# Swin block on one core: the second MLP layer in half precision, x in two tiles, K and Q ahead of the first MLP layer

## The chip, the core and the metric

The kernel runs on one NeuronCore of a Trainium2 chip. The core has five engines that work side by side and wait for each other through semaphores: TensorE (PE in the profile: matmuls and transposes; PEld is its weight load), VectorE (DVE), ScalarE (ACT), GpSimd (POOL) and SyncE (SP, which here only issues DMAs). Operands lie in SBUF, matmul results in eight banks of PSUM. The metric is the time of the program on the device in microseconds (us), the median of three runs.

## The reference

One Swin block with shifted windows, in float32: x is 32 images of 56 x 56 tokens with 128 channels.

```python
y = roll(layernorm(x) * g1 + b1, (-3, -3))                 # windows of 7 x 7 tokens, 16 heads of 8 channels
q, k, v = split(windows(y) @ qkv_w.T + qkv_b)
attn = softmax(q * 8**-0.5 @ k.T + rel_pos_bias + mask)
x1 = x + roll(unwindow((attn @ v) @ proj_w.T + proj_b), (3, 3))
h = gelu((layernorm(x1) * g2 + b2) @ fc1_w.T + fc1_b)     # 512 hidden channels, exact gelu
out = x1 + h @ fc2_w.T + fc2_b
```

## The kernel before

**Bands.** The work is cut into 128 bands (`STEPS`). A band is one row of 8 windows in two images: 7 x 112 = 784 tokens. Each tile holds a band, with tokens or channels on the partitions.

**Turns.** Every engine runs the same loop of turns, t = -2 to 130. In turn t it works on several bands at once, each in another stage: layernorm 1 of band t+2; transposed input, K and Q of band t+1, and the row maxima of its logits; V, logits, exp and the product with V of band t; attention output, projection, x1 and layernorm 2 of band t-1; the first MLP layer (fc1), gelu and four sevenths of the second (fc2) of band t-2; the last three sevenths of fc2 of band t-3. The order in a turn is written out by hand for each engine, and an engine never leaves it. A late operand therefore stops an engine and all that stands behind it.

**A turn on TensorE.** Transposes of z2 (L838), of the normalised x (L846) and of the maxima (L749). `fc2` of band t-3, rows 0 to 2 (L821). `fc1` chunks 0 and 1 (L805). K and Q (L867). `fc1` chunks 2 and 3. The spread of the softmax denominators (L881). V (L895). The projection (L904). Then the loop over eight windows w: `logits` (L771, L776), for even w `pv` (L791), for odd w one row of `fc2` (L821), and `max_logits` of the next band (L741), which with w = 0 waits for x1 (its PSUM banks 0 and 1 hold the projection until then) and with w > 0 for the maxima of w-1.

**Precision.** K, Q, V and fc1 use a split: a float32 operand is a high and a low float16 part, and three float16 products (high x high, low x high, high x low) replace one float32 product. fc2, the projection and the transposes are float32. Each float32 matmul shows as two passes, two records in the profile.

**VectorE in the middle of a turn.** `yT_lo` (L617, L621), the low part of the transposed x, which K and Q need; `sums` reciprocal (L630); the end of fc2 for three rows (L581); `norm1` of band t+2 (L521, L527), which waits for the x DMA; `k_lo` and `q_lo` (L641); `oT` (L657), attention output times the spread reciprocals; half of V into `v_own` (L672); x1 (L681) in two pieces; a second piece of V (L687); then the maxima (L589), one per window, with the statistics of layernorm 2 between them.

**ScalarE** makes `k_hi` and `q_hi` (L484), gelu (L438), two pieces of V (L500), exp (L421) and copies. **GpSimd** makes the low parts of the reciprocals (L372 to L378), the bias additions x_res (L384) and x1_b (L391), and both layernorms (`norm`, L350 to L361). **SyncE** issues the DMAs in order; x of band t+2 is loaded in turn t into the one tile `x_in`, after that tile's transposes.

The names k_hi, mx_k, st_q and so on in the rows are SBUF tiles; `ps` is PSUM.

Of the kernel before, what the change touches and what calls it, by code (L numbers as in the profile page):

```python
# [71 lines left out]
def swin_block_kernel(nc, x, wqT, wkT, wvT, wvpT, wpT, w1T, w2T, cols, rows, table_k, table_q, ident, eye,  # L72
# [11 lines left out]
    with ctx:  # L84
# [5 lines left out]
        w_2 = sb("w_2", [C, CH, C])  # L90
# [12 lines left out]
        x_in = sb("x_in", [TP, WS, C])  # L103
# [6 lines left out]
        z1, z2 = x_in, sb("z2", [TP, WS, C])  # L110
# [25 lines left out]
        hid = sb("hid", [C, CH, WS * TP])  # L136
# [4 lines left out]
        w_1, bv_wide = hid[:, 3, 0:HID], hid[:, 3, HID:HID + TP]  # L141
        w_q, w_k, w_v, w_vp = (oT_raw[:, k // 3, (k % 3) * C:(k % 3 + 1) * C] for k in range(4))
# [5 lines left out]
        def tokens_of(bank):  # L148
# [9 lines left out]
         s_h_lo, s_fc1, s_gelu, s_fc2, s_fin, s_stored, s_bd1, s_bd2, s_zero, s_init, s_initp, s_inita, s_bt,  # L158
# [11 lines left out]
                "h_high_ready", "h_low_ready", "fc1_done", "gelu_done", "fc2_done", "y_ready", "y_stored",  # L170
# [46 lines left out]
        def _(sp):  # L217
            band_dmas(sp, xr, x_in, 0, False, False, s_x)
# [30 lines left out]
            def body(t, edge, odd):  # L249
# [83 lines left out]
        def _(pool):  # L333
# [31 lines left out]
            def body(t, edge, odd):  # L365
                n = t - 1
                if exists(n):

                    pool.wait_ge(s_rsum, n + 1)
# [10 lines left out]
                    if n == 0:  # L380
                        pool.wait_ge(s_w, 16 * N_W)
                        pool.wait_ge(s_init, 2)
                    pool.wait_ge(s_xres_dma, loads(n, edge(n)))
                    nc.gpsimd.tensor_tensor(x_res[:, :, :], x_res[:, :, :],  # L384
                                            proj_b[:, :].unsqueeze(1).to_broadcast([TP, WS, C]),
                                            ALU.add).then_inc(s_xres, 1)
                n = t - 2
                if exists(n):
                    if past(n, 0):
                        pool.wait_ge(s_fin, 2 * n)  # L390
                    nc.gpsimd.tensor_tensor(x1_b[:, :, :], x1[:, :, :],  # L391
                                            fc2_b[:, :].unsqueeze(1).to_broadcast([TP, WS, C]),
                                            ALU.add).then_inc(s_x1b, 1)
                n = t + 2
                if exists(n):
                    norm(n, s_ln1, mv1, ve1, s_ve1, rs1, s_rs1, mr1, s_mr1, nm1, s_nm1, x_in, z1, s_t1, s_z1)
# [8 lines left out]
        def _(act):  # L405
# [27 lines left out]
            def gelu(n, c):  # L433
                if c == 0 and past(n, 0):
                    act.wait_ge(s_fc2, 2 * n)
                act.wait_ge(s_fc1, CH * n + c + 1)
                bank = 2 + 2 * (c % 2)
                nc.scalar.activation(hid[:, c, :].rearrange("p (b q) -> p b q", b=2), ps[:, bank:bank + 2, 0:HT],  # L438
                                     ACT.Gelu, bias=col[:, BF + c:BF + c + 1], scale=1 / W_SCALE).then_inc(s_gelu, 1)

            def body(t, edge, odd):
# [69 lines left out]
        def _(dve):  # L511
# [26 lines left out]
            norm1(0, lambda n: False)  # L538
# [21 lines left out]
            then(nc.vector.tensor_tensor(w1_lo[:, :], w_1, w1_hi[:, :], ALU.subtract))  # L560
            then(nc.vector.tensor_tensor(proj_b[:, :], proj_b[:, :], bp_ps, ALU.add))
# [33 lines left out]
            def body(t, edge, odd):  # L595
# [37 lines left out]
                n = t + 2  # L633
                if exists(n) and n != 0:
                    norm1(n, edge)
                n = t + 1
                if exists(n):
                    for j, (hi, lo, bank, b) in enumerate(((k_hi, k_lo, 0, BK), (q_hi, q_lo, 6, BQ))):
# [5 lines left out]
                        last.then_inc(s_lo, 1)  # L644
                n = t - 1
                if exists(n):
# [11 lines left out]
                    for im in range(2):  # L658
# [6 lines left out]
                        r[:, :, last_w, :, kept:WS].rearrange("p m i j -> p i m j")).then_inc(s_oT, 1)  # L665
                n = t
# [37 lines left out]

        @block.tensor
        def _(pe):
# [102 lines left out]
            def fc2(n, p, i):  # L809
                first, end = FC2_PARTS[p]  # L810
                if i == first and p == 1:
                    pe.wait_ge(s_gelu, CH * (n + 1))
                    if exists(n + 2):
                        pe.wait_ge(s_vown, 2 * (n + 2) + 1)
                        pe.wait_ge(s_vown_b, 2 * (n + 2) + 1)
                    elif n > 0:
                        pe.wait_ge(s_fin, 2 * n)
                if i == first and p == 0:
                    pe.wait_ge(s_fin, 2 * n + 1)
                for c in range(CH):  # L820
                    last = mm(ps[0:TP, 7, (i - first) * C:(i - first + 1) * C], hid[:, c, i * TP:(i + 1) * TP], w_2[:, c, :],  # L821
                              start=(c == 0), stop=(c == CH - 1))
# [3 lines left out]
            def body(t, edge, odd):  # L826
# [14 lines left out]
                if exists(n):  # L841
# [3 lines left out]
                    for i in range(WS):  # L845
                        last = nc.tensor.transpose(tokens_of(0)[:, i, 0:TP], z1[:, i, :], idn[0:TP, 0:TP])  # L846
# [22 lines left out]
                if exists(t - 2):  # L869
                    fc1(t - 2, 2)  # L870
# [108 lines left out]
```

## Time and profile before

| | |
|---|---|
| three runs | 4095.21 us (4090.11 to 4104.3) |
| the profiled execution | 4095.41 us, its span 4093.6 us |
| PE busy | 3947.3 us (96%), granted clock 0.995 |
| DVE busy | 2855.1 us (70%) |
| ACT busy | 2674.9 us (65%) |
| POOL busy | 2002.3 us (49%) |
| DMA | 35.6% of the 16 engines' time in the main queue |

PE shows 96% busy, but matmuls are pipelined, so the start times of matmuls in a turn, and not the busy share, tell how much time each piece occupies. The three other compute engines have idle time in each turn; what they cost is read where PE waits for them.

### The profile page before, as it was taken

The page shows a single profiled execution, that of the slowest core. Times are in us where ns is not written, and L with a number is a line of the kernel's source. Part 1 is how long each engine was busy: PE and PEld are TensorE (multiplying, and loading weights), DVE is VectorE, ACT ScalarE, POOL GpSimd, SP SyncE. Part 2 cuts the span into 40 slices and gives each one's busy share as a digit, 9 for nine tenths or more (in the row PEclk, how much of TensorE's full clock was granted, in tenths as well). Part 3 has the DMA queues.
Part 4 walks back from the last instruction along what each step waited for, and adds up shares of the span by engine and source line. Part 5 has one row for each costly group of instructions (what it writes and reads, how often), then busy time and mean ns, then how long its engine had stood idle before and what let it go on. Part 6 is the DMA issues. An engine that isn't in the chain of part 4 may idle for free. (4 is left out here: it accounts for less than half of the span.)

```text
span 4093.6 us, 168809 instructions
## 1 busy us (share of the span) xinstructions
PE 3947.3 (96%) x72080; PEld 3111.1 (76%) x72080; DVE 2855.1 (70%) x7453; ACT 2674.9 (65%) x3712; POOL 2002.3 (49%) x3476
## 2 busy tenths in 40 slices
PE   3899999999999999999999999999999999999998
PEld 2677777777777777777777777777777777777776
DVE  6677677677767777776776776777777667677764
ACT  1666666666666666666766666666666666666664
POOL 4454545445455454544544544454454445445453
PEclk8999999999999999999999999999999999999999
DMA  2333333333333333333333333333333333333332
GB/s 77 100 108 115 109 109 112 110 105 112 114 106 110 113 111 110 111 113 105 112 114 105 110 114 110 109 111 108 108 109 117 106 109 112 112 105 109 112 109 60
DMA packets 609568, 441.49 MB, mean 108 GB/s; under 512 B 142083, under 2 KB 608371, under 8 KB 608819
## 3 DMA queue, kind: packets, MB, share of 16 engines
q1 hardware_dynamic: 608355, 428.88, 35.6%
q8 instruction: 569, 9.32, 1.0%
q0 software_dynamic: 464, 1.81, 0.2%
q14 instruction: 180, 1.47, 0.1%
HBM read 106.14 MB, written 51.46 MB: 38 GB/s over the span
## 5 line engine op out<-in xcount | busy, mean ns | idle before, releaser
L589 DVE TENSOR_REDUCE neg_max<-ps 113x16 f32<-113x784 f32 x1024 | 995.9, 973 | 760.7 <-PE ps L741 760.5
L421 ACT ACTIVATE probs<-ps 113x784 f32<-113x784 f32 x1024 | 844.6, 825 | 858.4 <-PE ps L776 855.7
L821 PE MATMUL ps<-w,hid 128*112 128x128 f32 x7168 | 933.5, 279 | 1.9 <-ACT hid L438 1.0
L821 PEld LDWEIGHTS ps<-w,hid 128*112 128x112 f32 x7168 | 818.4, 177 | 81.9 <-issue 79.4
L776 PE MATMUL ps<-st_q,st_k 128*49 128x196 f16 x8192 | 696.2, 249 | 0.0
L771 PE MATMUL ps<-bias,eye_k 106*64 106x392 f16 x4096 | 686.5, 331 | 0.0
L438 ACT ACTIVATE hid<-ps,col 128x784 f32<-128x784 f32 x512 | 468.1, 915 | 165.4 <-PE ps L805 144.2
L741 PE MATMUL ps<-mx_k,mx_q 128*49 128x196 f16 x8192 | 544.2, 253 | 31.7 <-DMA mx_q<-q_hi 20.0
L350 POOL TENSOR_SCALAR ve<-mv 112x7 f32<-112x7 f32 x256 | 54.4, 212 | 1048.4 <-DVE mv L527 903.1
L776 PEld LDWEIGHTS ps<-st_q,st_k 128*49 128x49 f16 x8192 | 446.9, 105 | 122.0 <-issue 0.5
L372 POOL TENSOR_SCALAR r_hi<-sums 128x98 f16<-128x98 f32 x128 | 36.5, 285 | 897.9 <-DVE sums L630 897.9
L791 PE MATMUL ps<-probs,v_own 113*32 113x49 f32 x32768 | 464.4, 209 | 1.8 <-issue 1.5
L791 PEld LDWEIGHTS ps<-probs,v_own 113*32 113x32 f32 x32768 | 393.2, 110 | 83.6 <-issue 82.8
L741 PEld LDWEIGHTS ps<-mx_k,mx_q 128*49 128x49 f16 x8192 | 313.1, 103 | 152.1 <-DMA mx_q<-q_hi 33.1
L361 POOL TENSOR_SCALAR x_in<-x_in,rs,nm 112x128 f32<-112x128 f32 x896 | 389.5, 451 | 13.5 <-POOL nm L356 0.4
L361 POOL TENSOR_SCALAR z<-x,rs,nm 112x128 f32<-112x128 f32 x896 | 388.5, 449 | 13.4 <-POOL nm L356 0.3
L352 POOL TENSOR_TENSOR rs<-ve,half 112x7 f32<-112x7 f32 x256 | 380.4, 1486 | 21.3
L429 ACT ACTIVATE pv_sb<-ps 128x392 f32<-128x392 f32 x512 | 255.6, 499 | 203.9 <-PE ps L791 192.4
L414 ACT ACT_TABLE_LOAD x253 | 324.6, 1283 | 4.5
L521 DVE BATCH_NORM_STATS2 st<-x_in 112x6 f32<-112x128 f32 x896 | 185.9, 279 | 201.8 <-DMA x_in<-in_x 201.8
L384 POOL TENSOR_TENSOR x_res<-x_res,proj_b 112x896 f32<-112x896 f32 x128 | 267.2, 2088 | 10.3
L391 POOL TENSOR_TENSOR x_b<-x,fc_b 112x896 f32<-112x896 f32 x128 | 267.1, 2087 | 5.6 <-DVE y_out L581 5.6
(109 smaller groups left out, 6502.4 us busy)
## 6 DMA issues: line engine op xcount, KB each, us to landing
st_k<-k_hi SPq DMA_DIRECT2D x256, 196.0 KB
st_q<-q_hi SPq DMA_DIRECT2D x1024, 49.0 KB
oT_raw<-pv_sb SPq DMA_DIRECT2D x256, 196.0 KB, 3.6
x_in<-in_x SPq DMA_DIRECT2D x224, 196.0 KB
x_res<-in_x SPq DMA_DIRECT2D x224, 196.0 KB
out_y<-y_out SPq DMA_DIRECT2D x224, 196.0 KB
mx_k<-k_hi SPq DMA_DIRECT2D x512, 49.0 KB
mx_q<-q_hi SPq DMA_DIRECT2D x128, 196.0 KB
```

The lines of the kernel that those rows point to most:

```text
L352: nc.gpsimd.tensor_tensor(rs[:, :], ve[:, :], half[:, :], ALU.pow).then_inc(s_rs, 1)
L361: last = nc.gpsimd.tensor_scalar(z[:, i, :], src[:, i, :], rs[:, i:i + 1], nm[:, i:i + 1], ALU.mult, ALU.add)
L384: nc.gpsimd.tensor_tensor(x_res[:, :, :], x_res[:, :, :], proj_b[:, :].unsqueeze(1).to_broadcast([TP, WS, C]), ALU.add).then_inc(s_xres, 1)
L414: nc.scalar.activation(scrap[:, :], col[0:1, 0:1], function)
L421: nc.scalar.activation(probs[0:KP, w % 4, :].rearrange("p (b c) -> p b c", b=2), ps[0:KP, b:b + 2, 0:HB * WT], ACT.Exp).then_inc(s_exp, 1)
L438: nc.scalar.activation(hid[:, c, :].rearrange("p (b q) -> p b q", b=2), ps[:, bank:bank + 2, 0:HT], ACT.Gelu, bias=col[:, BF + c:BF + c + ...
L589: nc.vector.tensor_reduce(neg_max[0:KP, :, :, w].rearrange("p e g -> p g e"), ps[0:KP, 0:2, :].rearrange("p b (g c) -> p (b g) c", g=2)[:, ...
L741: last = mm(group(im, 0, g, 256), mx_q[edge(n)][:, g, span], mx_k[:, g, :, span], start=True, stop=True)
L771: mm(ps[HP * im:HP * (im + 1), bank + b, 0:HB * WT], eye_k[0:BIAS_ROWS, kind, im, :], bias[0:BIAS_ROWS, b, :], start=True, stop=False)
L776: last = mm(group(im, bank, g, EQ * WT), st_k[par][:, g, span], st_q[par][:, :, g, span], start=False, stop=(g % 2 == 1))
L791: last = mm(ps[32 * r:32 * r + VC, 6, first:first + WT], v_own[0:KP, w, h, :], probs[0:KP, w % 4, h * WT:(h + 1) * WT], start=True, stop=True)
L821: last = mm(ps[0:TP, 7, (i - first) * C:(i - first + 1) * C], hid[:, c, i * TP:(i + 1) * TP], w_2[:, c, :], start=(c == 0), stop=(c == CH ...
```

## The change

Five edits.

1. fc2 goes to half precision. Set-up splits w_2 (scaled by 64) into `w2_hi`, `w2_lo`. After each gelu chunk VectorE casts it to `hid_hi` (`hid_high`, four casts of 128 x 784 in a turn) and GpSimd subtracts to give `hid_lo` (four subtractions). TensorE does 12 float16 matmuls per row of fc2 where it did 4 float32 ones. The last step (`finish`) multiplies by 1/64 as it adds.
2. The float32 gelu output now shares its buffer with `probs`, the exp output, so exp of windows 0 to 3 waits for `hid_lo`.
3. K and Q move ahead of all four fc1 chunks on TensorE; on ScalarE all four gelus follow `k_hi` and `q_hi`.
4. x is held in two tiles and loaded a turn earlier (band t+3 in turn t). Its statistics move from the middle of the VectorE turn to the maxima of windows 4, 5 and 6, its moments to the end of the turn.
5. The second piece of V moves from VectorE to ScalarE, behind exp of window 0. On GpSimd the addition to x_res moves to the front of the turn.

```diff
-        w_2 = sb("w_2", [C, CH, C])
+        w2_hi, w2_lo = (sb(n, [C, CH, C], F16) for n in ("w2_hi", "w2_lo"))
-        x_in = sb("x_in", [TP, WS, C])
+        x_in = [sb(f"x_in{e}", [TP, WS, C]) for e in range(2)]
-        hid = sb("hid", [C, CH, WS * TP])
+        hid_hi, hid_lo = (sb(n, [C, CH, WS * TP], F16) for n in ("hid_hi", "hid_lo"))
+        hid = probs
...
 # SyncE
-                n = t + 2
-                if exists(n) and n != 0:
-                    sp.wait_ge(s_t1, n)
-                    band_dmas(sp, xr, x_in, n, edge(n), False, s_x)
+                n = t + 3
+                if exists(n):
+                    sp.wait_ge(s_st1, n)
+                    if past(n, 1):
+                        sp.wait_ge(s_t1, n - 1)
+                    band_dmas(sp, xr, x_in[odd(3)], n, edge(n), False, s_x)
...
 # GpSimd, after x1_b and ahead of norm of band t+2
+                n = t - 2
+                if exists(n):
+                    for c in range(CH):
+                        pool.wait_ge(s_hid_hi, CH * n + c + 1)
+                        nc.gpsimd.tensor_tensor(hid_lo[:, c, :], hid[:, c, :], hid_hi[:, c, :],
+                                                ALU.subtract).then_inc(s_hid_lo, 1)
...
 # ScalarE
+                if w < CH and exists(n - 2):
+                    act.wait_ge(s_hid_lo, CH * (n - 2) + w + 1)
...
+                        if w == 0:
+                            nc.scalar.activation(v_place(0, 1), v_made(0, 1), ACT.Copy).then_inc(s_vown_b, 1)
...
 # VectorE
+            then(nc.vector.tensor_scalar(w_2, w_2, W_SCALE, None, ALU.mult))
+            then(nc.vector.tensor_copy(w2_hi[:, :, :], w_2))
+            then(nc.vector.tensor_tensor(w2_lo[:, :, :], w_2, w2_hi[:, :, :], ALU.subtract))
...
+            def hid_high(n, c):
+                dve.wait_ge(s_gelu, CH * n + c + 1)
+                if c == 0 and past(n, 0):
+                    dve.wait_ge(s_fc2, 2 * n)
+                nc.vector.tensor_copy(hid_hi[:, c, :], hid[:, c, :]).then_inc(s_hid_hi, 1)
...
-                n = t + 2
-                if exists(n) and n != 0:
-                    norm1(n, edge)
...
 # VectorE, after q_lo
+                if exists(t - 2):
+                    hid_high(t - 2, 0)
+                    hid_high(t - 2, 1)
...
 # VectorE, after oT
+                if exists(t - 2):
+                    hid_high(t - 2, 2)
+                    hid_high(t - 2, 3)
...
 # TensorE, fc2
-                for c in range(CH):
-                    last = mm(ps[0:TP, 7, (i - first) * C:(i - first + 1) * C], hid[:, c, i * TP:(i + 1) * TP], w_2[:, c, :],
-                              start=(c == 0), stop=(c == CH - 1))
+                for c in range(CH):
+                    for w_part in (w2_hi, w2_lo):
+                        mm(row, hid_hi[:, c, i * TP:(i + 1) * TP], w_part[:, c, :],
+                           start=(c == 0 and w_part is w2_hi), stop=False)
+                for c in range(CH):
+                    if i == first and p == 1:
+                        pe.wait_ge(s_hid_lo, CH * n + c + 1)
+                    last = mm(row, hid_lo[:, c, i * TP:(i + 1) * TP], w2_hi[:, c, :], start=False, stop=(c == CH - 1))
```

The order on TensorE after fc2 of band t-3, first before the change (L805 is fc1, two chunks; L867 is K and Q):

```order
L821 MATMUL ps<-w,hid 112x128 x11
L805 MATMUL ps<-h_hi,w_hi 128x392 [waits h_low_ready]
L805 MATMUL ps<-h_hi,w_hi 128x392
L805 MATMUL ps<-h_lo,w_hi 128x392 x2
L805 MATMUL ps<-h_hi,w_lo 128x392 x2
L805 MATMUL ps<-h_hi,w_hi 128x392 [waits exp_done]
L805 MATMUL ps<-h_hi,w_hi 128x392
L805 MATMUL ps<-h_lo,w_hi 128x392 x2
L805 MATMUL ps<-h_hi,w_lo 128x392 x2
L867 MATMUL ps<-yT_hi,wk_hi 128x392 [waits y_low_ready]
```

and the same place after it (L860 is the end of fc2, L902 is K and Q, L837 is fc1):

```order
L860 MATMUL ps<-w_hi,hid_lo 112x128 x4
L902 MATMUL ps<-yT_hi,wk_hi 128x392 [waits y_low_ready]
L902 MATMUL ps<-yT_hi,wk_hi 128x392
L902 MATMUL ps<-yT_lo,wk_hi 128x392 x2
L902 MATMUL ps<-yT_hi,wk_lo 128x392 x2
L902 MATMUL ps<-yT_hi,wq_hi 128x392 [waits y_ready,neg_maxT_ready]
L902 MATMUL ps<-yT_hi,wq_hi 128x392
L902 MATMUL ps<-yT_lo,wq_hi 128x392 x2
L902 MATMUL ps<-yT_hi,wq_lo 128x392 x2
L837 MATMUL ps<-h_hi,w_hi 128x392 [waits h_low_ready]
```

K and Q, with their wait for `yT_lo`, now stand directly behind fc2; the 12 matmuls of two fc1 chunks that stood between them are behind Q.

VectorE from q_lo to the first maxima, before (L657 is oT, L672 and L687 are pieces of V, L681 is x1):

```order
L641 SCALAR_TENSOR_TENSOR q_lo<-ps,col,q_hi 128x8x49
L657 TENSOR_TENSOR oT<-oT_raw,ps 128x7x49 [waits projected,r_spread,o_in]
L657 TENSOR_TENSOR oT<-oT_raw,ps 128x7x49
L657 TENSOR_TENSOR oT<-oT_raw,ps 128x14x4
L657 TENSOR_TENSOR oT<-oT_raw,ps 128x14x3
L672 COPY v_own<-ps 49x512 [waits v_projected,pv_done]
L681 TENSOR_TENSOR x<-ps,x_res 112x512 [waits projected,x1_biased,x_res_biased]
L681 TENSOR_TENSOR x<-ps,x_res 112x384 [waits projected]
L687 COPY v_own<-ps 49x512 [waits v_projected,x1_ready]
L589 TENSOR_REDUCE neg_max<-ps 113x4x4 [waits max_transposed,max_logits_ready]
```

and after (L604 is hid_high, `probs` is the buffer of the gelu output):

```order
L604 CAST hid_hi<-probs 128x784 [waits fc2_done,gelu_done]
L604 CAST hid_hi<-probs 128x784 [waits gelu_done]
L678 TENSOR_TENSOR oT<-oT_raw,ps 128x7x49 [waits projected,r_spread,o_in]
L678 TENSOR_TENSOR oT<-oT_raw,ps 128x7x49
L678 TENSOR_TENSOR oT<-oT_raw,ps 128x14x4
L678 TENSOR_TENSOR oT<-oT_raw,ps 128x14x3
L604 CAST hid_hi<-probs 128x784 [waits gelu_done] x2
L696 COPY v_own<-ps 49x512 [waits v_projected,pv_done]
L705 TENSOR_TENSOR x<-ps,x_res 112x512 [waits projected,x1_biased,x_res_biased]
L705 TENSOR_TENSOR x<-ps,x_res 112x384 [waits projected]
L610 TENSOR_REDUCE neg_max<-ps 113x4x4 [waits max_transposed,max_logits_ready,x1_ready]
```

Two casts stand ahead of oT and two between oT and x1; the piece of V behind x1 is gone from this engine.

GpSimd in a turn after the change:

```order
L377 TENSOR_TENSOR x_res<-x_res,proj_b 112x896 [waits x_res_loaded]
L383 TENSOR_SCALAR r_hi<-sums 128x98 [waits r_rows_in,r_sums_ready]
L386 TENSOR_TENSOR sums<-sums,r_hi 128x98 [waits r_high_ready]
L389 TENSOR_SCALAR r_lo<-sums 128x98 [waits r_rest_ready]
L395 TENSOR_TENSOR x_b<-x,fc_b 112x896 [waits y_ready]
L402 TENSOR_TENSOR hid_lo<-probs,hid_hi 128x784 [waits hid_high_ready] x4
L354 TENSOR_SCALAR ve<-mv 112x7 [waits moments1_done]
```

The four subtractions stand between x1_b and layernorm 1, where there was nothing before.

## Rows read from the trace of the kernel before

**Rows 1.** Source view of L749; columns: engine, form, count, ns min/median/max, first and last start.

```profile
L749 PE MATMUL ps<-idn,neg_max x128: 262/262/395, 81.6 to 4024.6; 113*128 113x113 f32 x128
```

**Rows 2.** Timeline of one turn, PE; columns: start, us, engine, line, operation, count, idle before.

```profile
2002.91 0.26 PE L749 MATMUL ps<-idn,neg_max 113*128 113x113 f32 x1
2002.91 2.68 PEld L821 LDWEIGHTS ps<-w,hid 128*112 128x112 f32 x24
...
2005.53 0.21 PEld L805 LDWEIGHTS ps<-h_hi,w_hi 128*128 128x128 f16 x2
...
2007.62 0.50 PE L867 MATMUL ps<-yT_hi,wk_hi 128*128 128x392 f16 x2
...
2009.67 0.49 PE L805 MATMUL ps<-h_hi,w_hi 128*128 128x392 f16 x2
...
2010.66 0.49 PE L805 MATMUL ps<-h_hi,w_hi 128*128 128x392 f16 x2
...
2011.75 0.50 PE L881 MATMUL ps<-r_rows,sel 32*128 32x392 f16 x2
2012.28 0.10 PEld L895 LDWEIGHTS ps<-wv_hi,yT_hi 128*128 128x128 f16 x1 [0.42 <-DVE q_lo L641]
...
2013.58 1.58 PEld L904 LDWEIGHTS ps<-w_p,oT 128*112 128x112 f32 x14
...
2015.29 0.11 PEld L771 LDWEIGHTS ps<-bias,eye_k 106*64 106x64 f16 x2
...
2016.12 0.33 PEld L741 LDWEIGHTS ps<-mx_k,mx_q 128*49 128x49 f16 x8 [0.18 <-issue]
...
2017.29 0.93 PEld L821 LDWEIGHTS ps<-w,hid 128*112 128x112 f32 x8 [0.16 <-issue]
...
2018.35 0.30 PEld L741 LDWEIGHTS ps<-mx_k,mx_q 128*49 128x49 f16 x8
...
2033.56 0.26 PE L749 MATMUL ps<-idn,neg_max 113*128 113x113 f32 x1
```

**Rows 3.** Waits in total: who waited for what, us, times, longest.

```profile
DVE st L521 <- DMA x_in<-in_x: 201.8, 128, 2.8
```

**Rows 4.** Timeline of the same turn, DVE.

```profile
2005.26 0.34 DVE L621 TENSOR_TENSOR yT_lo<-ps,yT_hi 128x56 f16<-128x56 f32 x2
...
2010.03 1.13 DVE L641 SCALAR_TENSOR_TENSOR k_lo<-ps,col,k_hi 128x392 f16<-128x392 f32 x2
2011.08 1.15 DVE L641 SCALAR_TENSOR_TENSOR q_lo<-ps,col,q_hi 128x392 f16<-128x392 f32 x2
2012.34 1.17 DVE L657 TENSOR_TENSOR oT<-oT_raw,ps 128x343 f32<-128x343 f32 x4
2013.42 1.06 DVE L672 COPY v_own<-ps 49x512 f32<-49x512 f32 x1
2014.85 1.16 DVE L681 TENSOR_TENSOR x<-ps,x_res 112x512 f32<-112x512 f32 x2 [0.36 <-PE ps L904]
```

**Rows 5.** Timeline of the same turn, ACT.

```profile
2006.89 1.85 ACT L438 ACTIVATE hid<-ps,col 128x784 f32<-128x784 f32 x2 [1.10 <-PE ps L805]
...
2008.93 0.93 ACT L484 ACTIVATE k_hi<-ps,col 128x784 f16<-128x784 f32 x1 [0.19 <-PE ps L867]
```

**Rows 6.** Timeline of the same turn, POOL.

```profile
2009.59 2.09 POOL L391 TENSOR_TENSOR x_b<-x,fc_b 112x896 f32<-112x896 f32 x1
...
2014.22 3.04 POOL L361 TENSOR_SCALAR x_in<-x_in,rs,nm 112x128 f32<-112x128 f32 x7
```

**Rows 7.** Groups by line, POOL; count, then busy us, mean ns, idle before.

```profile
L375 POOL TENSOR_TENSOR sums<-sums,r_hi 128x98 f32<-128x98 f32 x128 | 47.5, 371 | 10.7
```

**Rows 8.** Timeline of the set-up, DVE and POOL.

```profile
21.12 14.30 DVE L546 COPY v_own<-own 113x128 f32<-113x128 f32 x2 [8.50 <-DMA fc_b<-in_rows]
...
37.82 3.97 POOL L361 TENSOR_SCALAR x_in<-x_in,rs,nm 112x128 f32<-112x128 f32 x7
...
40.05 0.56 DVE L559 CAST w_hi<-hid 128x512 f16<-128x512 f32 x1
...
41.82 0.57 DVE L564 CAST hid<-hid 128x784 f16<-128x784 f32 x1
```

More of the change, by code:

```diff
@@ L367, in body @@
                 if exists(n):
+                    if n == 0:
+                        pool.wait_ge(s_w, 16 * N_W)
+                        pool.wait_ge(s_init, 2)
+                    pool.wait_ge(s_xres_dma, loads(n, edge(n)))
+                    nc.gpsimd.tensor_tensor(x_res[:, :, :], x_res[:, :, :],
+                                            proj_b[:, :].unsqueeze(1).to_broadcast([TP, WS, C]),
+                                            ALU.add).then_inc(s_xres, 1)
                     pool.wait_ge(s_rsum, n + 1)
@@ L379, in body @@
                                             ALU.mult, ALU.add).then_inc(s_r_lo, 1)
[L380 to L386, printed above, removed]
                 n = t - 2
@@ L433, in gelu @@
             def gelu(n, c):
-                if c == 0 and past(n, 0):
-                    act.wait_ge(s_fc2, 2 * n)
                 act.wait_ge(s_fc1, CH * n + c + 1)
@@ L473, in body @@
                     load_table(ACT.Gelu)
-                    gelu(t - 2, 0)
-                    gelu(t - 2, 1)
                 n = t + 1
@@ L487, in body @@
                 if exists(t - 2):
+                    gelu(t - 2, 0)
+                    gelu(t - 2, 1)
                     gelu(t - 2, 2)
@@ L528, in aggregate, with moments1 @@
                 last.then_inc(s_mv, 1)
-            def norm1(n, edge):
-                dve.wait_ge(s_x, loads(n, edge(n)))
+            def moments1(n):
                 if past(n, 0):
                     dve.wait_ge(s_z1, n)
-                stats(x_in, st1, (0, WS)).then_inc(s_st1, 1)
                 aggregate(n, st1, s_st1, mv1, s_ln1)
             nc.vector.memset(hid[:, 0:2, :], 0.0).then_inc(s_zero, 1)
-            norm1(0, lambda n: False)
+            dve.wait_ge(s_x, loads(0, False))
+            stats(x_in[0], st1, (0, WS)).then_inc(s_st1, 1)
+            moments1(0)
             nc.vector.memset(bv_wide, 0.0)
@@ L580, in finish @@
                 dve.wait_ge(s_fc2, 2 * n + 2 - p)
-                nc.vector.tensor_tensor(y_out[:, i0:i1, :],
-                                        ps[0:TP, 7, 0:(i1 - i0) * C].rearrange("p (i c) -> p i c", c=C),
-                                        x1_b[:, i0:i1, :], ALU.add).then_inc(s_fin, 1)
+                nc.vector.scalar_tensor_tensor(
+                    y_out[:, i0:i1, :], ps[0:TP, 7, 0:(i1 - i0) * C].rearrange("p (i c) -> p i c", c=C),
+                    1 / W_SCALE, x1_b[:, i0:i1, :], ALU.mult, ALU.add).then_inc(s_fin, 1)
+            def hid_high(n, c):
[3 more added lines that the diff above has]
+                nc.vector.tensor_copy(hid_hi[:, c, :], hid[:, c, :]).then_inc(s_hid_hi, 1)
             def row_maxima(n, w):
@@ L699, in body @@
                             aggregate(n, st2, s_st2, mv2, s_ln2)
+                    n = t + 3
+                    if exists(n):
+                        if w == 4:
+                            dve.wait_ge(s_x, loads(n, edge(n)))
+                            stats(x_in[odd(3)], st1, (0, 1))
+                        if w == 5:
+                            stats(x_in[odd(3)], st1, (1, 4))
+                        if w == 6:
+                            stats(x_in[odd(3)], st1, (4, WS)).then_inc(s_st1, 1)
                 if exists(t - 2):
                     finish(t - 2, 1, edge)
+                if exists(t + 3):
+                    moments1(t + 3)
             turns(body)
@@ L782, in pv @@
                 if u == 0:
-                    pe.wait_ge(s_vown, 2 * n + 2)
-                    pe.wait_ge(s_vown_b, 2 * n + 2)
+                    pe.wait_ge(s_vown, n + 1)
+                    pe.wait_ge(s_vown_b, 3 * (n + 1))
                 else:
@@ L811, in fc2 @@
                 if i == first and p == 1:
-                    pe.wait_ge(s_gelu, CH * (n + 1))
+                    pe.wait_ge(s_hid_hi, CH * (n + 1))
                     if exists(n + 2):
-                        pe.wait_ge(s_vown, 2 * (n + 2) + 1)
-                        pe.wait_ge(s_vown_b, 2 * (n + 2) + 1)
+                        pe.wait_ge(s_vown, n + 3)
+                        pe.wait_ge(s_vown_b, 3 * (n + 2) + 1)
                     elif n > 0:
@@ L819, in fc2 @@
                     pe.wait_ge(s_fin, 2 * n + 1)
+                row = ps[0:TP, 7, (i - first) * C:(i - first + 1) * C]
                 for c in range(CH):
-                    last = mm(ps[0:TP, 7, (i - first) * C:(i - first + 1) * C], hid[:, c, i * TP:(i + 1) * TP], w_2[:, c, :],
-                              start=(c == 0), stop=(c == CH - 1))
+                    for w_part in (w2_hi, w2_lo):
[5 more added lines that the diff above has]
+                    last = mm(row, hid_lo[:, c, i * TP:(i + 1) * TP], w2_hi[:, c, :], start=False, stop=(c == CH - 1))
                 if i == end - 1:
@@ L845, in body @@
                     for i in range(WS):
-                        last = nc.tensor.transpose(tokens_of(0)[:, i, 0:TP], z1[:, i, :], idn[0:TP, 0:TP])
+                        last = nc.tensor.transpose(tokens_of(0)[:, i, 0:TP], x_in[odd(1)][:, i, :], idn[0:TP, 0:TP])
                     last.then_inc(s_t1, 1)
@@ L869, in body @@
                 if exists(t - 2):
+                    fc1(t - 2, 0)
+                    fc1(t - 2, 1)
                     fc1(t - 2, 2)
```

18 lines of the change are left out of this document (6 added, 12 removed).

## The prediction

> **What bounds the kernel now.** I read the page's engine shares first (PE 96%, the others 70% and less), then the starts of the transpose L749, which stands once in each turn: 81.6 to 4024.6 us with 127 turns between, 31.05 us each [rows 1]. Nearly the whole time is 127 times one turn, so I then read one quiet turn from the timeline, 2002.91 to 2033.56 us, 30.65 us long [rows 2]. The reader is to see that PE goes from piece to piece in it with short gaps: it waits for q_lo ahead of V (0.42 us at the weight load), and for little else. Others are longer. The likely source is the late x DMA: VectorE waits for it in every turn, 201.8 us in all and at most 2.8 at once [rows 3], and k_lo, q_lo and so V are behind that wait. The mean turn has 0.40 us of this over the quiet one. So PE's order is the bound, and the change is worth what it does to PE's start times in a turn. I write times of the quiet turn from here without the 2000.
>
> **Edit 1, fc2 on PE.** A float32 pass takes 0.109 us: 24 passes fill 2.91 to 5.53 [rows 2]. A float16 matmul of the same 128 columns with its own weight load is seen in V: 24 of them fill 12.28 to 13.58, 0.054 us each. The three early rows go from 24 x 0.109 = 2.62 us to 36 x 0.054 = 1.95, a gain of 0.67. In the window loop one row stands between 17.29 and 18.35: 1.06 us for 8 passes, of which 0.87 is passes and 0.19 the change of shapes [rows 2]. After, 12 x 0.054 = 0.65 plus 0.19 if that stays (gain 0.22), plus nothing if it goes (0.41). I take 0.28, nearer the first, for all shape changes on PE seem to pay it; four rows give 1.1 us (0.9 to 1.6).
>
> **Edit 3, K and Q first.** fc2 would end at 5.53 - 0.67 = 4.86, but K and Q need yT_lo, which ends at 5.26 + 0.34 = 5.60 [rows 4]. Nothing in the change moves it. So K starts at 5.7 and the 0.67 is lost in a wait. Before, two fc1 chunks covered that time. K and Q take 9.67 - 7.62 = 2.05, so fc1 starts at 7.75, with 0.99 a chunk [rows 2]: 7.75, 8.74. k_hi starts 1.31 behind K's first matmul (8.93 - 7.62) [rows 2, 5], at 7.0, q_hi at 7.95 to 8.88. Then come the gelus, 0.93 each (1.85 for two [rows 5]), the first at 9.0: ends 9.95 and 10.9, then about 12.2 and 13.1, behind chunks 2 and 3. Chunk 2 needs the banks of gelu 0 and starts at 10.0, chunk 3 at 11.0. The spread follows at about 12.05, where it stood at 11.75, and V at 12.4 instead of 12.28. The V wait for q_lo goes (q_lo now ends at 8.0 + 2.2 = 10.2 [rows 4]), and the fc1 waits take its place: up to V this edit and the first give nothing, -0.1.
>
> **Edit 1 on VectorE and GpSimd, the dear part.** An uncontended cast of 128 x 784 took 0.57 us in the set-up [rows 8]; behind another DVE instruction it takes about 0.5. A subtraction on GpSimd: 2.09 us at 896 elements and 0.37 at 98 give 2.15 ns per element [rows 6, 7], so 1.85 at 784. Four are 7.4 us a turn on an engine with half its time idle, and four casts 2.0 on VectorE, where the x statistics that left the middle of the turn had stood ahead of k_lo. By busy time both fit. The question is what they do to each other.
>
> **The trace on casts beside GpSimd.** In steady state before no SBUF to SBUF cast runs beside GpSimd work. The set-up has it. Seven GpSimd normalisations take 3.97 us there beside casts and 3.04 in a turn without [rows 6, 8]. The cast of 512 elements inside that stretch takes 0.56 us, as long as the cast of 784 behind it. And the first copy of v_own, which starts under GpSimd's memsets, stays open for 14.3 us [rows 8]. So a cast and a GpSimd instruction hold each other up; with the pieces of PSUM input (oT, V, x1) no such stretch shows. What a cast pays if a 1.85 us subtraction has begun lies between 0 and the rest of that subtraction plus some 0.4. I take the whole rest, as in the set-up both sides lengthen.
>
> The Trainium skill says the same and stronger ("SBUF — State Buffer", section Who interferes with whom): a VectorE cast from SBUF to SBUF can run in a mode that uses the port pair shared with GpSimd, the pair is locked for a whole instruction, and the other side blocks fully. By it the sum is the one below; without it, the sum of the first rival.
>
> **The chain to the window loop.** Cast 0 runs 10.2 to 10.75 (x1_b, moved up with the x_res addition gone to the front, ends at 9.6). Subtraction 0 runs 10.85 to 12.7. Cast 1 has its gelu at 10.9, is held to 12.7 and ends at 13.1. oT stands behind it on VectorE: 13.1 to 14.25, where it was 12.34 to 13.51 [rows 4]. The projection waits for oT and starts at 14.3, not 13.58; logits 0 at 16.0, not 15.29. Subtraction 1 runs 13.15 to 15.0. Cast 2 is held to it and ends at 15.4, cast 3, already queued, at 15.9. Then the V piece 0.98 (1.06, starts overlap by 0.08), then x1 1.16, end 17.95. max_logits 0 waits for x1: it starts at 18.05, where it was 16.12 [rows 2]. Delay 1.9 us. Behind the waiting instruction on PE stand logits 1, all of fc2, pv and the maxima; nothing can pass.
>
> Subtractions 2 and 3 end at 17.7 and 19.6. The first late row of fc2 starts 1.17 behind max_logits 0, at 19.2, and needs subtraction 3 some 0.6 later, at 19.8: just in time. Exp 0 to 3 wait for the same and are later still. The V piece moved to ScalarE (1.06) ends near 18.9, ahead of exp 1's logits: free. GpSimd's norms end 8 us after the subtractions where they have until the next turn: free.
>
> **Edit 4.** The x DMA gets a turn of lead, so the 0.40 us of jitter goes; the bound is 0 to 0.40 and I take all, since max_logits also waits 1.9 us longer for its own operands. The statistics between the last maxima hide under PE (16.12 to 18.35, 2.23 us from the first maxima to the second [rows 2], against 0.98 for a reduction and some 0.7 for three statistics).
>
> **Sum.** Quiet turn 30.65 + 1.9 - 1.1 = 31.45 against the mean 31.05: +0.40, times 127 = +51 us. Once: three more set-up operations like the cast of 0.56, +1.9; and in the last two turns no attention work covers the four subtractions, 7.4 us in each, of which I take 6 in all. +8. From the profiled execution, 4095.4 (0.2 above the median of the runs, so the same): 4154 us.
>
> **Rivals.** Free pair (0.28): a cast doesn't wait for GpSimd. Cast 1 ends at 11.5, oT at 13.8, casts 2 and 3 at 14.85, V piece 15.8, x1 16.9, max_logits 0 at 17.0: delay 0.88. Turn 30.65 + 0.88 - 1.1 = 30.43, -0.62 x 127 = -79, +8: 4024, the faster side. It decides by one thing, whether casts 1 and 2 last over 1 us. For it: GpSimd's x_res and x1_b additions never stretch in steady state; against it: the set-up rows.
>
> Half a hold (0.15): a cast waits only 0.7 us each time. Delay some 1.4, turn 30.95, 4091.
>
> GpSimd takes the next subtraction ahead of cast 3 (0.07): cast 3 waits 1.85 more, as the v_own copy stayed behind several memsets. +235: 4389.
>
> The forecast has 0.50, own range 4115 to 4195 (0.3 us a turn is 38 us). A clock that falls by PE's new pauses (0.7, 0.3, 0.5, 1.2 us) I leave out: none is long, and the clock is 0.995 granted over the run.
>
> **How the numbers follow.** Within 0.3% (12 us) no change can be told. Forecast case: 0.85 slower, 0.10 same, 0.05 faster. Free pair: faster. Half: 0.40 faster, 0.40 same, 0.20 slower. Last: slower. Sums 0.365, 0.11, 0.525. Range 4000 to 4200: the two main cases with a little more.
>
> **What would show it.** Right: L604 casts with a mean over 1 us, casts 1 and 2 near 2 us; GpSimd subtractions 1.85 us; PE waits on x1 ahead of max_logits 0 over 1 us and on yT_lo 0.7; no DVE wait on the x DMA; fc2 matmuls 0.054 apart. Wrong: casts all at 0.57, or PE waits for hid_lo or exp in the loop, or a loop that gains under 0.9 us.

## The result and the profile after

The changed kernel takes 4127.39 us (median of six runs, 4117.75 to 4134.01) against 4093.22 for the kernel before on the same chip. The ratio is 1.008, interval 1.0063 to 1.0097: slower by 34 us, with the whole interval above 1. The forecast was 4154. The profiled execution took 4126.65 us.

The page of the changed kernel, engine shares:

```profile
PE 3818.7 (93%) x75664; PEld 2928.0 (71%) x75664; DVE 3198.2 (78%) x7840; ACT 2803.9 (68%) x3840; POOL 2905.1 (70%) x3988
```

PE has 129 us less to do and GpSimd 903 us more. The turn, as in [rows 1] (source view of the transpose of the maxima, now L781):

```profile
L781 PE MATMUL ps<-idn,neg_max x128: 262/262/395, 83.4 to 4048.7; 113*128 113x113 f32 x128
```

(4048.7 - 83.4) / 127 = 31.22 us, where it was 31.05. 127 turns of 0.17 to 0.18 are 22 us; another 9 us lie once at the ends. Together they are the 31 us between the two profiled executions (4126.65 and 4095.41).

One turn of the changed kernel, PE, to be read against [rows 2]:

```profile
2019.51 0.26 PE L781 MATMUL ps<-idn,neg_max 113*128 113x113 f32 x1
...
2022.26 0.51 PE L902 MATMUL ps<-yT_hi,wk_hi 128*128 128x392 f16 x2 [0.48 <-DVE yT_lo L642]
...
2028.68 0.50 PE L918 MATMUL ps<-r_rows,sel 32*128 32x392 f16 x2
...
2030.54 1.78 PE L941 MATMUL ps<-w_p,oT 128*112 128x128 f32 x14
2032.25 0.36 PE L803 MATMUL ps<-bias,eye_k 106*64 106x392 f16 x2
...
2034.18 0.53 PE L773 MATMUL ps<-mx_k,mx_q 128*49 128x196 f16 x8 [1.06 <-DVE x L705]
```

Counted from the transpose that opens the turn, max_logits 0 (L773) starts at 14.67 us. Its row in the kernel before is

```profile
2016.15 0.53 PE L741 MATMUL ps<-mx_k,mx_q 128*49 128x196 f16 x8
```

and 16.15 - 2.91 = 13.24 us. It now waits 1.06 us for x1. The same turn on VectorE, against [rows 4]:

```profile
2026.67 0.56 DVE L604 CAST hid_hi<-probs 128x784 f16<-128x784 f32 x1
2027.56 1.85 DVE L604 CAST hid_hi<-probs 128x784 f16<-128x784 f32 x1 [0.33 <-ACT probs L448]
2029.33 1.15 DVE L678 TENSOR_TENSOR oT<-oT_raw,ps 128x343 f32<-128x343 f32 x4
2030.40 1.66 DVE L604 CAST hid_hi<-probs 128x784 f16<-128x784 f32 x2
2031.98 1.07 DVE L696 COPY v_own<-ps 49x512 f32<-49x512 f32 x1
2032.90 1.14 DVE L705 TENSOR_TENSOR x<-ps,x_res 112x512 f32<-112x512 f32 x2
```

and on GpSimd, against [rows 6]:

```profile
2024.14 2.09 POOL L395 TENSOR_TENSOR x_b<-x,fc_b 112x896 f32<-112x896 f32 x1
2027.31 1.67 POOL L402 TENSOR_TENSOR hid_lo<-probs,hid_hi 128x784 f16<-128x784 f32 x1 [1.08 <-DVE hid_hi L604]
2029.48 1.68 POOL L402 TENSOR_TENSOR hid_lo<-probs,hid_hi 128x784 f16<-128x784 f32 x1 [0.50 <-DVE hid_hi L604]
2031.66 3.57 POOL L402 TENSOR_TENSOR hid_lo<-probs,hid_hi 128x784 f16<-128x784 f32 x2 [0.50 <-DVE hid_hi L604]
```

Lay the two side by side. Cast 0 takes 0.56 us with GpSimd idle. Cast 1 begins at 2027.56, inside the subtraction that runs from 2027.31 to 2028.98, and ends at 2029.41, 0.43 us behind it. Cast 2 begins inside the next subtraction (2029.48 to 2031.16) and takes 1.18 us, to 2031.58, again 0.42 us behind it. Cast 3 begins right behind it, ahead of the next subtraction, and takes 0.56 us; the pair ends at 2032.06 instead of some 2031.4. The third subtraction begins under cast 3 and takes 1.94 us. Over the run (groups by line: busy time in us, mean in ns, then the wait before):

```profile
L402 POOL TENSOR_TENSOR hid_lo<-probs,hid_hi 128x784 f16<-128x784 f32 x512 | 887.3, 1745 | 263.2 <-DVE hid_hi L604 263.2
L604 DVE CAST hid_hi<-probs 128x784 f16<-128x784 f32 x512 | 518.1, 1032 | 44.3 <-ACT probs L448 44.3
```

and the waits that answer to [rows 3]:

```profile
PE ps L773 <- DVE x L705: 132.7, 124, 1.2
...
PE ps L902 <- DVE yT_lo L642: 68.6, 128, 2.5
```

A cast has a mean of 1.03 us, and PE's wait for x1, which was 0.3 us in the whole run before, is 1.07 us a turn. VectorE's wait for the x DMA, 201.8 us before, is 2.3 us.

### The profile page after: what moved, and what is told of

Read it like the earlier page. It is cut to its first block and busy times, and to the rows that moved or that the text cites. A ratio compares the mean times of both kernels' runs of the same rounds, so it can differ in the third digit from the quotient of the medians.

```text
span 4124.8 us, 177003 instructions
## 1 busy us (share of the span) xinstructions
PE 3818.7 (93%) x75664; PEld 2928.0 (71%) x75664; DVE 3198.2 (78%) x7840; ACT 2803.9 (68%) x3840; POOL 2905.1 (70%) x3988
## 5 line engine op out<-in xcount | busy, mean ns | idle before, releaser
L402 POOL TENSOR_TENSOR hid_lo<-probs,hid_hi 128x784 f16<-128x784 f32 x512 | 887.3, 1745 | 263.2 <-DVE hid_hi L604 263.2
L773 PE MATMUL ps<-mx_k,mx_q 128*49 128x196 f16 x8192 | 543.8, 253 | 149.5 <-DVE x L705 132.7
L604 DVE CAST hid_hi<-probs 128x784 f16<-128x784 f32 x512 | 518.1, 1032 | 44.3 <-ACT probs L448 44.3
L855 PE MATMUL ps<-w_hi,hid_hi 128*112 128x128 f16 x3584 | 521.7, 226 | 4.3 <-DVE hid_hi L604 3.5
L448 ACT ACTIVATE probs<-ps,col 128x784 f32<-128x784 f32 x512 | 468.4, 915 | 69.3 <-PE ps L837 40.3
L855 PE MATMUL ps<-w_lo,hid_hi 128*112 128x128 f16 x3584 | 499.0, 220 | 0.0
L773 PEld LDWEIGHTS ps<-mx_k,mx_q 128*49 128x49 f16 x8192 | 313.8, 103 | 240.6 <-issue 139.5
L855 PEld LDWEIGHTS ps<-w_hi,hid_hi 128*112 128x112 f16 x3584 | 417.6, 130 | 84.4 <-issue 79.5
L855 PEld LDWEIGHTS ps<-w_lo,hid_hi 128*112 128x112 f16 x3584 | 419.1, 131 | 0.0
L860 PE MATMUL ps<-w_hi,hid_lo 128*112 128x128 f16 x3584 | 348.8, 220 | 1.9 <-POOL hid_lo L402 1.9
```

The source lines that it names most:

```text
L402: nc.gpsimd.tensor_tensor(hid_lo[:, c, :], hid[:, c, :], hid_hi[:, c, :], ALU.subtract).then_inc(s_hid_lo, 1)
L604: nc.vector.tensor_copy(hid_hi[:, c, :], hid[:, c, :]).then_inc(s_hid_hi, 1)
L773: last = mm(group(im, 0, g, 256), mx_q[edge(n)][:, g, span], mx_k[:, g, :, span], start=True, stop=True)
L855: mm(row, hid_hi[:, c, i * TP:(i + 1) * TP], w_part[:, c, :], start=(c == 0 and w_part is w2_hi), stop=False)
```

## The experiments

Each ratio is to the kernel before on the same chip. The kernels ran on different chips, so two of them are best compared by their ratios; 0.01 of the ratio is 41 us. A mean turn is the span between the first and last of the 128 transposes, over 127. The quiet turn is the length that the shortest steady turns share (their fifth percentile). The diffs are abridged.

**Small subtractions.**

```diff
-  nc.gpsimd.tensor_tensor(hid_lo[:, c, :], hid[:, c, :], hid_hi[:, c, :], ALU.subtract)
+  nc.gpsimd.memset(hid_lo[:, :, :], 0.0)      # set-up
+  nc.gpsimd.tensor_tensor(hid_lo[:, c, 0:16], hid[:, c, 0:16], hid_hi[:, c, 0:16], ALU.subtract)
```

> The changed kernel with each GpSimd subtraction cut from 784 to 16 columns (the rest of hid_lo stays zero, so most of the low part of fc2 is left out); casts, order and PE work as they are. Theory (a cast waits for the subtraction that runs): cast 1 falls from 1.85 to 0.57 us, cast 2 from 1.18 to 0.57, so casts 2 and 3 end 0.6 us earlier and x1 and max_logits 0 with them; oT moves by at most 0.1, since the spread bounds it too. Turn 31.22 - 0.6, tail - 6 us: about 4045 us. Rival (casts are long for another reason, or only their number on VectorE counts): casts stay at a mean of 1.03 us, 4120 to 4127 us.

Measured: 4037.62 us, ratio 0.987 (0.9849 to 0.9891). Mean turn 30.54 us, 0.68 below the changed kernel. The casts:

```profile
L605 DVE CAST hid_hi<-probs 128x784 f16<-128x784 f32 x512 | 277.6, 563 | 44.4 <-ACT probs L449 44.3
```

The same 512 casts at the same places take 0.563 us instead of 1.032. oT kept its place, as expected: in this order the spread bounds it as closely as cast 1 does (it starts at 9.77 us instead of 9.82 in the median turn). max_logits 0 starts 0.69 us earlier, and the rest of the turn is as long as it was. So the hold is worth some 86 us (0.68 x 127), and without it the change would have been faster, as the first rival had it (4024). The hold of cast 2 is the one that delays x1; that of cast 1 counts because subtraction 1, which holds cast 2, can only start when cast 1 is done.

**The cast in a slower form.**

```diff
-  nc.vector.tensor_copy(hid_hi[:, c, :], hid[:, c, :])
+  nc.vector.tensor_reduce(hid_hi[:, c, :], hid[:, c, :].unsqueeze(2), AX_X, ALU.max)
```

> The changed kernel with each cast done as a tensor_reduce over an axis of length 1, which works at one element a cycle. Theory (only the fast two-element form of the cast and GpSimd hold each other up): every cast takes 0.98 us whatever GpSimd does, subtraction 2 falls from 1.94 to 1.68, oT keeps its place, casts 2 and 3 end 0.25 us later than now: 4160 us. Rival (any VectorE read of SBUF waits for GpSimd): casts 1 and 2 take over 1.8 us, max_logits 0 is 0.9 us later, about 4240 us.

Measured: 4136.87 us, ratio 1.0108 (1.0088 to 1.0128).

```profile
L604 DVE TENSOR_REDUCE hid_hi<-probs x512: 955/959/971, 148.2 to 4121.8; 128x784 f16<-128x784 f32 x171
```

```profile
L402 POOL TENSOR_TENSOR hid_lo<-probs,hid_hi x512: 1662/1681/1697, 149.2 to 4124.5; 128x784 f16<-128x784 f32 x171
```

These are two source views, ns as min/median/max. No reduction of the 512 is longer than 0.971 us and no subtraction longer than 1.697, where the changed kernel has 2.055. The hold belongs to the form of the instruction, not to VectorE reading SBUF. The kernel does not gain by it, for each cast is now 0.40 us longer: max_logits 0 starts at 14.81 us in the median turn, against 14.69. The Trainium skill ("SBUF — State Buffer", Who interferes with whom) counts tensor_reduce on this chip among the operations that never contend; the trace agrees.

**Two x tiles alone**, on the kernel before (edit 4 and nothing else).

```diff
-  x_in = sb("x_in", [TP, WS, C])
+  x_in = [sb(f"x_in{e}", [TP, WS, C]) for e in range(2)]   # loads and statistics as in the changed kernel
```

> The kernel before with edit 4 alone (two x tiles, x a turn earlier, statistics between the maxima). Theory (the 0.43 us by which the mean turn exceeds the quiet one comes from the late x DMA and from the DMA of mx_q): the x part, about half, goes; VectorE's wait for x falls from 201.8 us to near 0; quiet turn unchanged at 30.62, 4055 to 4070 us, mean turn about 30.8. Rival (the spread between turns has another source): 4093 us.

Measured: 4073.22 us, ratio 0.9957 (0.9937 to 0.9976); mean turn 30.79. Waits:

```profile
PEld ps L752 <- DMA mx_q<-q_hi: 36.5, 60, 5.0
...
DVE st L523 <- DMA x_in<-in_x: 2.6, 1, 2.6
```

The x wait is gone with 0.26 of the 0.43 us. What is left between turns is the DMA of mx_q, for which the matmuls themselves wait 22.3 us in all, 0.18 a turn. The median lies 3 us above the forecast range.

**Edit 3 undone.**

```diff
+  fc1(t - 2, 0); fc1(t - 2, 1)        # behind fc2 of band t-3, ahead of K and Q; gelu 0 and 1 ahead of k_hi
   ...K and Q...
-  fc1(t - 2, 0); fc1(t - 2, 1)
```

> The changed kernel with edit 3 alone undone: fc1 chunks 0 and 1 and gelu 0 and 1 stand ahead of K and Q again, casts 0 and 1 still behind q_lo. Theory: the PE wait for yT_lo (0.7 us) goes, V starts 0.8 to 1.0 us earlier, but GpSimd can start its four subtractions only when the casts behind q_lo are done; max_logits 0 comes 0.5 us earlier and the first late fc2 row then waits some 1.0 us for subtraction 3. Turn about 31.6, 4190 us. Rival (PE order is all that counts): turn 30.6, 4050 us.

Measured: 4359.6 us, ratio 1.065 (1.0625 to 1.0675), mean turn 33.06. The sign was right and the size short by 170 us. PE did get to V nearly 1 us earlier, but max_logits 0 came 0.9 us later and not 0.5 earlier. VectorE, and GpSimd beside it:

```profile
2007.95 1.03 DVE L604 CAST hid_hi<-probs 128x784 f16<-128x784 f32 x2
2008.90 1.15 DVE L678 TENSOR_TENSOR oT<-oT_raw,ps 128x343 f32<-128x343 f32 x4
2009.97 2.93 DVE L604 CAST hid_hi<-probs 128x784 f16<-128x784 f32 x2
2012.82 1.06 DVE L696 COPY v_own<-ps 49x512 f32<-49x512 f32 x1
```

```profile
2008.58 7.48 POOL L402 TENSOR_TENSOR hid_lo<-probs,hid_hi 128x784 f16<-128x784 f32 x4 [2.44 <-DVE hid_hi L604]
```

Casts 0 and 1 run back to back and are both done long before subtraction 0 ends, so GpSimd has subtraction 1 ready to go. It takes turns with the casts: cast 2 goes after subtraction 0, cast 3 only after subtraction 1. The pair of casts takes 2.93 us and max_logits 0 waits:

```profile
2015.01 0.53 PE L773 MATMUL ps<-mx_k,mx_q 128*49 128x196 f16 x8 [2.32 <-DVE x L705]
```

That pause has a price of its own (windows view; the column after POOL is the granted clock):

```profile
2010.00:2015.00 5.00, 2.59 (x26) 2.13 (x27) 4.86 (x6) 4.04 (x5) 5.00 (x4) 1.00 0.63 191
2015.00:2018.50 3.50, 3.49 (x42) 3.04 (x44) 1.37 (x4) 0.82 (x1) 3.17 (x5) 0.67 0.31 115
2018.50:2022.00 3.50, 3.50 (x102) 2.64 (x99) 2.28 (x5) 1.50 (x3) 3.05 (x8) 0.84 0.34 118
```

Behind the 2.3 us pause the clock is at its lower level, 1.2 GHz, for a part of the time, although PE works without a gap there. Mean clock over this run: 0.962, against 0.993. The 37 turns without such a stretch, of 127, have a median of 32.0 us; the median of all is 33.5. The mean turn is 1.46 us above the forecast 31.6: about 1.07 of it (33.06 - 31.99) is the clock. In the rest, max_logits 0 is 1.4 us later than forecast, by cast 3, while the wait of 1.0 us for subtraction 3 did not come (4.5 us in the whole run). The last two experiments keep fc1 first without the long pause; in the first of them the clock stays at its upper level from 124 to 3920 us of the run, in the second there is one short stretch at the lower.

**Casts 2 and 3 behind x1, with its control.**

```diff
-  hid_high(t - 2, 2); hid_high(t - 2, 3)      # behind oT
+  hid_high(t - 2, 2); hid_high(t - 2, 3)      # behind x1
...
-  if exists(t - 2) and w % 2: fc2(t - 2, 1, FC2_PARTS[1][0] + w // 2)
+  if exists(t - 2) and w in (3, 5, 6, 7): ...  # the control has only these two lines
```

> The changed kernel with casts 2 and 3 behind x1 on VectorE, and the four late fc2 rows at windows 3, 5, 6, 7 instead of 1, 3, 5, 7. Theory (max_logits 0 is late only by what stands between oT and x1): max_logits 0 at 13.6 instead of 14.69; but window 1 has no fc2 row under which the maxima of window 0 hide, so 0.6 to 0.7 of the gain goes there. Turn 30.7, 4060 to 4080 us. Rival (the x1 chain has another bound): max_logits 0 stays at 14.7, turn 31.8, 4200 us.

> The changed kernel with the four late fc2 rows at windows 3, 5, 6, 7 alone, casts in their place: the control for e3_casts_behind_x1. Theory (the row at window 1 covers the reduction of window 0): max_logits 0 stays at 14.7, window 1 loses 0.5 to 0.7 us, turn 31.7 to 31.9, about 4200 us; the casts behind x1 are then worth over 100 us against it. Rival (subtraction 3 holds up the row at window 1, so moving it helps): 4127 us or less.

Measured: 4078.0 us, ratio 0.9965 (0.9951 to 0.998), and for the control 4180.28, ratio 1.0225 (1.0199 to 1.0251). With x1 ahead of the casts, max_logits 0 starts 13.6 us into the turn instead of 14.69, and the move is worth 102 us against the control. That x1's place behind the casts sets max_logits 0 is thereby shown; the move takes out the casts' own time together with their hold, for behind x1 they meet no subtraction (0.57 us each). The row at window 1 is worth some 53 us where it stood: it covers the reduction of window 0, for which PE waits 65.7 us in the control and 10.6 in the changed kernel.

**fc2 back in float32**, edits 3 to 5 kept.

```diff
-  hid = probs                      # hid_hi, hid_lo, casts, subtractions, w2_hi, w2_lo
+  hid = sb("hid", [C, CH, WS * TP])
-  12 float16 matmuls a row
+  mm(ps[...], hid[:, c, i * TP:(i + 1) * TP], w_2[:, c, :], start=(c == 0), stop=(c == CH - 1))
```

> The changed kernel with edit 1 and 2 undone: fc2 in float32, its own gelu buffer, no casts, no subtractions; edits 3, 4, 5 kept. Theory (edit 1 gives 1.0 us in the loop and takes it back, and more, ahead of it): K and Q start at 2.75 as in the changed kernel, max_logits 0 follows logits 0 at 13.6, the loop takes its old 17.4 us. Turn 31.0 to 31.1, 4095 us, that is 30 us below the changed kernel. Rival (half precision pays somewhere not seen): slower than the changed kernel, over 4150 us.

Measured: 4116.37 us, ratio 1.0059 (1.0044 to 1.0074), mean turn 31.20. The quiet turn is 31.02, as expected, but the mean is 0.18 more; Q waits for the end of fc2 in 37 turns, 10.7 us in all, which is about half of that. So the run is only some 10 us below the changed kernel, where 30 were forecast. Edits 3 to 5 alone thus cost 25 us, though edit 4 alone gains 15 to 18: edits 3 and 5 together cost about 40 us in float32. They were not tried apart. V, ahead of which only edit 3 changes the order on PE, starts at 9.67 us in the median turn, 0.40 later than in the kernel with edit 4 alone (9.27). Half precision on top of it adds some 10 us: behind max_logits 0 it takes 0.9 us off the mean turn (17.41 to 16.52), ahead of it it adds 0.9 (13.79 to 14.71).

**The order that the experiments point to.** fc1 first again, gelus 0 and 1 ahead of k_hi, casts 0 and 1 in the slower form ahead of k_lo, casts 2 and 3 plain behind oT.

```diff
+  fc1(t - 2, 0); fc1(t - 2, 1)        # ahead of K and Q, as in the kernel before
+  hid_high(t - 2, 0); hid_high(t - 2, 1)      # ahead of k_lo
+  if c < 2: nc.vector.tensor_reduce(hid_hi[:, c, :], hid[:, c, :].unsqueeze(2), AX_X, ALU.max)
```

> The changed kernel with edit 3 undone (fc1 chunks 0 and 1 and gelu 0 and 1 ahead of K and Q), casts 0 and 1 ahead of k_lo as tensor_reduce over an axis of length 1 (0.96 us, never held in the run with all casts so), casts 2 and 3 behind oT as plain casts. Theory (the order with fc1 first lost only because casts and subtractions met): subtractions 0 and 1 run under K, Q and V and end near 10.1 us behind L781's start, casts 2 and 3 then run nearly free (about 0.6 us each), max_logits 0 at 13.15 us instead of 14.69, no PE pause over 0.8 us and no lower clock. Turn 29.6 to 29.7, 3935 us. Rival (fc1 first is itself what costs, by some other wait): no better than 4127.

Measured: 3949.93 us, ratio 0.9656 (0.964 to 0.9673), mean turn 29.93: faster than both kernels. GpSimd and VectorE in one turn:

```profile
2004.73 2.09 POOL L395 TENSOR_TENSOR x_b<-x,fc_b 112x896 f32<-112x896 f32 x1
2006.76 3.32 POOL L402 TENSOR_TENSOR hid_lo<-probs,hid_hi 128x784 f16<-128x784 f32 x2
```

```profile
2003.98 1.97 DVE L605 TENSOR_REDUCE hid_hi<-probs 128x784 f16<-128x784 f32 x2
...
2009.63 1.35 DVE L607 CAST hid_hi<-probs 128x784 f16<-128x784 f32 x2
```

The two reductions run straight through x1_b at 0.97 us each. Subtractions 0 and 1 are over at 2010.08, and casts 2 and 3 lose 0.3 us here; in the median turn the pair takes 1.04 us and loses nothing. PE's longest wait for an operand is now the transfer of mx_q, for which its weight loads waited 33 us in the kernel before (the matmuls themselves: 20.0 before, 63.6 now):

```profile
PEld ps L776 <- DMA mx_q<-q_hi: 116.6, 126, 5.0
```

**The same with all casts plain**, the diff against the run just shown.

```diff
-  if c < 2: nc.vector.tensor_reduce(...)
+  nc.vector.tensor_copy(hid_hi[:, c, :], hid[:, c, :])
```

> The kernel of e5_mixed with casts 0 and 1 as plain casts (the fast form) in the same place ahead of k_lo, all else the same. Theory (a plain cast is held by whatever GpSimd runs): cast 1, ready at 5.2 us behind L781's start, is held by the x1_b addition (4.6 to 6.7) and ends near 7.1, so k_lo, q_lo and V are 0.6 to 0.8 us later than in e5_mixed: turn 30.6, about 4035 us. Rival (the slower form of the cast is not needed in this place): casts of 0.57 us, 3950 us or a little less.

Measured: 4034.56 us, ratio 0.9865 (0.9844 to 0.9885), mean turn 30.51. VectorE and GpSimd:

```profile
2015.64 2.30 DVE L604 CAST hid_hi<-probs 128x784 f16<-128x784 f32 x1 [0.43 <-ACT probs L448]
```

```profile
2015.43 2.08 POOL L395 TENSOR_TENSOR x_b<-x,fc_b 112x896 f32<-112x896 f32 x1
```

Cast 1 meets x1_b and takes 2.30 us instead of 0.57; k_lo, q_lo and V stand behind it, and V starts at 9.74 us in the median turn instead of 8.66. A form that takes 0.97 us instead of 0.57 makes the kernel 85 us faster.

## Why the prediction was right

**The mechanism** was the one forecast: casts and subtractions hold each other up, x1 comes late, max_logits 0 waits over 1 us. Removing either side of it (small subtractions, the other form of cast) takes the hold away, and the all-plain run brings it back at another place. The other theory, that only the number of instructions on VectorE counts, is excluded by the small subtractions: as many casts, some 86 us less. The slower form alone does not pay, since its own time replaces the hold; it pays in the order that stands last but one, where it keeps k_lo on time.

**The chain, term by term**, from the start of the turn. Cast 1 ended at 9.90 (forecast 10.19), casts 2 and 3 at 12.07 and 12.55 (12.49 and 12.99), x1 at 14.53 (15.04), max_logits 0 at 14.67 (15.14). The delay was some 1.45 us, forecast 1.9. The term that was mis-sized is the subtraction: 1.68 us, not the 1.85 drawn from two float32 results; it counts twice, 0.34 of the 0.47. The rest is a start 0.13 earlier. Without the hold the first rival had a delay of 0.88, so the forecast gave the hold 1.0 us; the small subtractions put it at 0.69.

**Where the chain was read wrong.** The forecast put oT behind cast 1, and with it the projection 0.7 us later (11.39 from the start of the turn) and logits 0 at 13.09. Measured: 11.03 and 12.74, and without any hold 10.99 and 12.70. So cast 1 hardly delays oT; what delays it and V is the later spread (9.17, against 8.84 in a quiet turn before). This did not spoil the sum, because x1 waits for cast 2 and cast 2 for subtraction 1. The evidence from the set-up was also thinner than it was taken for: of the seven normalisations, 0.44 us each when undisturbed, the one beside the cast of 512 elements took 0.61 and one beside a float32 subtraction on VectorE 0.87. The rows showed that the two engines disturb each other, and not how long a cast of this kind is held; that it is the whole rest of the subtraction was an assumption, which the runs bore out.

**The gain in the loop** was 1.0 us in a quiet turn (17.4 from max_logits 0 to the end of the turn before, 16.4 after) and 0.9 in the mean (17.41 and 16.52), forecast 1.1. The early rows gained nothing, as forecast: PE waits for yT_lo, 0.54 us in the mean.

**Edit 4.** I took all 0.40 us of jitter as gone. The changed kernel keeps 0.13 (quiet turn 31.09, mean 31.22), and the run with edit 4 alone 0.17. This step failed in part: in the kernel before only the x share goes with the x DMA, and the rest is the wait for mx_q. The changed kernel's 0.13 is another: PE waits only 6.1 us for mx_q in it, and 0.11 of the 0.13 lies in the window loop, which is 0.3 to 1.1 us longer than 16.41 in 15 of the 127 turns. The quiet turn was 0.36 us better than forecast and the jitter 0.13 worse: 0.23 x 127 = 29 us, the whole difference between 4154 and the profiled 4126.65. In part the two errors cancel, and that is luck: the forecast change was +59 us, the measured one +34, or +31 between the profiled executions.

**Once.** 8 us forecast, 9 measured.

**Edit 3** with the early rows was put at -0.1 us up to V. V started at 9.61, where it was 9.37 in the turn shown: -0.24. Part of the miss is the wait for q_lo ahead of V, which was read as 0.42 us at the weight load; V's first matmul stood 0.53 us behind the spread with it and stands 0.44 behind it without, so it was worth 0.1. The float32 run shows the same cost of the new order, or more. And I had not seen what edit 3 prevents. With fc1 first and the casts where they are, GpSimd gets ahead of cast 3 and the clock falls: 4359.6 us, 232 worse. The rival in which GpSimd goes ahead of cast 3 (4389) did not occur in the changed kernel and did occur there.

**Left open.** Why cast 3, queued behind cast 2, goes ahead of a subtraction that waits for cast 2's semaphore is only argued (the semaphore comes late); it was not tried apart. The 0.17 us of jitter by the mx_q transfer was not removed, and the source of the longer window loops in the changed kernel was not looked for. Edits 3 and 5 were not tried apart, nor was K and Q first with the casts of the fastest kernel. In the run with fc1 first, the long pause and the lower clock come together; that the pause is the cause rests on the runs without it.

## What to carry to other kernels

Before work is split between VectorE and GpSimd, ask of each pair of instructions that may overlap whether it can hold the other up; free time on both engines says nothing of it. A held instruction costs through what is queued behind it, so put a cast where GpSimd is idle, or give it a slower form that is not held. When PE's order is changed, look at which other engine's start it moves: K and Q first was better by 232 us with the casts where this change puts them, edits 3 and 5 together cost some 40 us in float32, and the fastest kernel here has fc1 first with the casts moved.

## What the runs showed of the hardware

- A float32 to float16 cast of 128 x 784 in SBUF takes 0.56 us; begun during a GpSimd instruction it ends some 0.4 us after that one (1.85 us beside a subtraction and 2.30 beside the x1_b addition). A GpSimd subtraction is held in return, 1.94 to 2.05 us instead of 1.68.
- The two sides take turns when both are ready (cast 2, subtraction 1, cast 3 with fc1 first: the pair of casts takes 2.93 us), but in the changed kernel a cast queued directly behind a cast goes ahead of a subtraction that still waits for its semaphore (the pair takes 1.66 us).
- A GpSimd subtraction float32 minus float16 to float16 took 0.22 us at 16 columns and 1.68 at 784, which makes 1.90 ns per column; the float32 additions of the kernel before made 2.15.
- tensor_reduce over an axis of length 1 casts 128 x 784 in 0.96 to 0.97 us and is neither held nor holds (512 of 512).
- A PE pause of 2.3 us in each turn went with stretches at 1.2 GHz in 90 of 127 turns, and pauses of 1.1 us with none between 147 and 4058 us of the run: mean clock 0.962 against 0.993.
